# Key and value projections of a windowed attention moved into the steps of the compressed attention

## What is computed

```python
y_cmp = _mha(Q, blk, blk, ...[0])          # every query against 49 block means
y_sel = _mha(Q, K_sel, K_sel, ...[1])      # every query against the 4 best blocks
padded = jnp.pad(feat, ((0, 0), (pad, pad), (pad, pad), (0, 0)), mode='edge')
q = _lin(Q, wq_w[2], wq_b[2])              # query projection
k = _lin(patches, wk_w[2], wk_b[2])        # key projection, of padded positions
v = _lin(patches, wv_w[2], wv_b[2])        # value projection, of padded positions
attn = jax.nn.softmax(jnp.einsum('bnhd,bnwhd->bnhw', q, k) * scale, axis=-1)
y_win = _lin(jnp.einsum('bnhw,bnwhd->bnhd', attn, v).reshape(Bx, Nq, C), pj_w[2], pj_b[2])
g = jax.nn.softmax(_lin(_ln(Q, n1_w, n1_b), g_w, g_b), axis=-1)     # three gates per query
y = g[..., 0:1] * y_cmp + g[..., 1:2] * y_sel + g[..., 2:3] * y_win + Q
```

## Time and profile before

| | us |
|---|---|
| median of 3 runs (lowest, highest) | 842.41 (840.88, 844.82) |
| the profiled execution | 849.34 |
| its span | 847.5 |
| projection loop, first product to last | 92.12 to 224.4 |
| end of the gates | 234.5 |
| compressed attention, first maximum to last addition | 236.92 to 387.1 |
| windowed attention, then MLP | to 847.5 |

### The profile page before, as it was taken

How to read it: one execution, slowest core, us unless ns; L and a number is a source line. 1 busy time by engine, 2 the same in 40 slices (tenths; PEclk the granted TensorE clock), 3 DMA queues, 4 the chain that set the end, 5 groups by cost and what they waited for, 6 DMA issues and landing times.

```text
span 847.5 us, 14128 instructions
## 1 busy us (share of the span) xinstructions
PE 718.2 (85%) x5053; PEld 374.7 (44%) x5053; DVE 623.4 (74%) x1260; ACT 354.4 (42%) x609; POOL 201.4 (24%) x323
## 2 busy tenths in 40 slices
PE   4937966877489999997899899999988999999993
PEld 2525532333134444444455555555534545455551
DVE  6976445555677999996767767777729889999960
ACT  2160224434423344341445454454561351546566
POOL 1010122323324444440610010010056046600000
PEclk9966798999867999997799999999999999999998
DMA  5000055555588000001455665665100000000000
GB/s 223 0 1 0 19 141 126 143 145 135 139 201 220 1 0 1 2 0 56 124 147 142 164 172 135 173 165 150 37 4 1 0 0 1 1 19 20 38 39 38
DMA packets 52519, 66.22 MB, mean 78 GB/s; under 512 B 10590, under 2 KB 48226, under 8 KB 50594
## 3 DMA queue, kind: packets, MB, share of 16 engines
q1 hardware_dynamic: 49282, 43.08, 19.0%
q10 hardware_dynamic: 3168, 22.24, 9.5%
HBM read 43.03 MB, written 21.57 MB: 76 GB/s over the span
## 4 chain that ended last, share of the span: by engine, by line
PE 40%; DVE 20%; issue 5%; DMA 5%; ACT 4%; SPq 0%; POOL 0%; ACTq 0%; DVEq 0%
PE banks L870 12%; PE banks L810 5%; PE banks L794 5%; PE banks L772 4%; DVE mx L1241 4%; DVE sm L1254 3%; DMA Q<-nT 3%; PE banks L825 3%; DVE AC L1073 2%; DVE wn L1298 2%; DVE sm L1256 2%; DVE X L1326 2%; DMA FP<-nT 1%; PE banks L711 1%; PE banks L756 1%
## 5 line engine op out<-in xcount | busy, mean ns | idle before, releaser
L972 ACT ACTIVATE P<-banks 126x480 f32<-126x480 f32 (+2 forms) x196 | 100.2, 521 | 126.4 <-PE banks L794 102.3
L1298 DVE TENSOR_REDUCE wn<-banks 128x4 f32<-128x728 f32 x112 | 102.0, 914 | 40.6 <-PE banks L772 39.5
L870 PE MATMUL banks<-FP,PTB 128*128 128x392 f32 x384 | 129.5, 493 | 2.1 <-DVE c L1329 1.2
L1073 DVE SCALAR_TENSOR_TENSOR AC<-XT,vec,AC 128x1540 f32<-128x1540 f32 (+5 forms) x48 | 117.9, 2461 | 1.1
L870 PEld LDWEIGHTS banks<-FP,PTB 128*128 128x128 f32 x384 | 72.7, 190 | 56.8 <-DVE FP L1367 2.1
L501 POOL TENSOR_TENSOR SEB<-SEB,rg 112x392 f32<-112x392 f32 x112 | 58.3, 541 | 90.2 <-DVE rg L1261 90.1
L485 POOL TENSOR_TENSOR pk<-pr,pk 128x434 bf16<-128x434 f32 (+1 forms) x42 | 42.7, 1018 | 136.7 <-DVE pk L1181 136.7
L810 PE MATMUL banks<-P,Vw 126*17 126x120 f32 (+2 forms) x1568 | 74.3, 263 | 0.0
L1170 DVE TENSOR_TENSOR pr<-pf,pk 128x434 f32<-128x434 f32 (+1 forms) x42 | 31.9, 760 | 57.1 <-ACT pk L927 56.6
L951 ACT ACTIVATE SEB<-SEB 112x424 f32<-112x424 f32 x56 | 31.2, 557 | 89.8 <-DVE SEB L1244 89.8
L731 PE MATMUL banks<-PTB,VP 106*128 106x448 f32 x112 | 54.2, 572 | 5.1 <-ACT PTB L960 5.1
(11 more groups left out here) (228 smaller groups left out, 1255.3 us busy)
## 6 DMA issues: line engine op xcount, KB each, us to landing
k_parts<-pk SPq DMA_DIRECT2D x84, 108.5 KB, 2.8
Vw<-v_rows SPq DMA_DIRECT2D x84, 66.9 KB
q_parts<-pk SPq DMA_DIRECT2D x42, 112.0 KB, 2.7
K<-k_parts ACTq DMA_DIRECT2D x7, 651.0 KB, 6.0
v_rows<-vst SPq DMA_DIRECT2D x14, 263.5 KB
X<-in_x SPq DMA_DIRECT2D x2, 1568.0 KB, 8.1
out_y<-zs SPq DMA_DIRECT2D x8, 392.0 KB, 2.3
K<-k_parts ACTq DMA_DIRECT2D x7, 434.0 KB, 3.6
```

The costliest lines, as they stand in the source:

```text
L870: last = mm(bank(2 + place_in_unit, C, ZPIX), WT[:, dy, part, C * grp:C * (grp + 1)], D[:, part, QROWS * q + dy:QROWS * (q + 1) + dy, :].r ...
L972: a(P[q % 4][0:BKEYS[b], 0:4 * BQ[b]], PS[0:BKEYS[b], 4 + q % 2, 0:4 * BQ[b]], ACT.Exp).then_inc(sem("w_exp"), 1)
L1073: return ve.scalar_tensor_tensor(out=o, in0=src(ro + dy, rn, co + dx, cn), scalar=v(wcol + t), in1=o, op0=ALU.mult, op1=ALU.add)
L1298: ve.tensor_reduce(dst, src, AX.X, ALU.max, negate=True).then_inc(sem("w_slot_read"), 1)
```

## The change

The order of `pjobs` is turned round: 14 query jobs come first, then the 28 key jobs. Only the query jobs stay ahead of the compressed attention, one with each gate job. The loop there has 16 turns: in turn n, query job n and gate job n begin, gate job n-1 gets its two products, and gate job n-2 is transposed. The 28 key jobs are handed out over the first 40 of the 56 steps (`late_at[14 + n] = n * 40 // 28`, so in steps 0, 1, 2, 4, 5, 7, 8, 10, ...), always into bank 6. 16 of these steps also carry a value job (steps 0, 1, 4, 7, 10, 11, 14, 17, 20, 21, ...), in bank 7. For the job of step k, PE multiplies at the end of its step k, ACT reads at the end of its step k, DVE subtracts at the start of its step k+1 and rounds at its end (behind the value rows), and POOL makes the third part in its step k+2. SP stores these 28 jobs after it has spread the gate rows, and loads the first three bands after that. POOL clears borders only after its last step.

```diff
-        pjobs = [(m, "k", h * KBAND // 2, KBAND // 2) for m in range(IMAGES) for h in range(2 * BANDS)]
-        pjobs += [(m, "q", b * BAND, BAND) for m in range(IMAGES) for b in range(BANDS)]
+        pjobs = [(m, "q", b * BAND, BAND) for m in range(IMAGES) for b in range(BANDS)]
+        pjobs += [(m, "k", h * KBAND // 2, KBAND // 2) for m in range(IMAGES) for h in range(2 * BANDS)]
...
-        VPLACES = sorted([3 * k + 1 for k in range(NGJ)] + [2, 5])
+        NLATE = NPJ - NGJ
+        LATE_STEPS = 40
+        late_at = {NGJ + n: n * LATE_STEPS // NLATE for n in range(NLATE)}
+        vlate_at = {late_at[NGJ + j * 7 // 4]: j for j in range(NVJ)}
+        VPLACES = [NGJ + j * 7 // 4 for j in range(NVJ)]
...
-        PBANKS = (5, 6, 3)
+        PBANKS = (5, 7, 3)
+        LATE_BANK = 6
...
+                    for n in late_jobs(CB * i + k - 2):
+                        third_part(n)
...
-            c_body(0, False)
+            for i in range(BANDS):
+                c_body(i, False)
+            c_body(BANDS, True)
             pool.wait_ge(sem("proj"), NPJ)
...
-            for i in range(1, BANDS):
-                c_body(i, False)
-            c_body(BANDS, True)
...
+                    step = CB * i + k
+                    for n in late_jobs(step):
+                        pe.wait_ge(sem("proj_read"), n)
+                        if n == NGJ:
+                            pe.wait_ge(sem("g_rows"), 1)
+                        project(n, LATE_BANK)
+                    if step in vlate_at:
+                        values(vlate_at[step])
...
+                    for n in late_jobs(CB * i + k):
+                        first_parts(n, LATE_BANK)
...
+                    for n in late_jobs(CB * i + k - 1):
+                        residual(n)
...
+                    if CB * i + k - 1 in vlate_at:
+                        value_rows(vlate_at[CB * i + k - 1])
+                    for n in late_jobs(CB * i + k - 1):
+                        second_part(n)
```

More of the change, by code:

```diff
@@ L277, in build, with late_jobs @@
         NGJ = len(gjobs)
-        assert NPJ == 3 * NGJ
-        VPLACES = sorted([3 * k + 1 for k in range(NGJ)] + [2, 5])
-        assert len(VPLACES) == NVJ
+        NLATE = NPJ - NGJ
[3 more added lines that the diff above has]
+        VPLACES = [NGJ + j * 7 // 4 for j in range(NVJ)]
+        assert len(vlate_at) == NVJ and len(set(VPLACES)) == NVJ
+        def late_jobs(step):
+            return [n for n, at0 in late_at.items() if at0 == step]
         PEB = 5
-        PBANKS = (5, 6, 3)
+        PBANKS = (5, 7, 3)
+        LATE_BANK = 6
         CT = IMAGES * BANDS * TILES
@@ L381, in _, with store_parts @@
             sp.dma_start(pjrow[:], pjb).then_inc(sem("loaded"), 16)
-            for n, (m, which, at0, cols) in enumerate(pjobs):
+            def store_parts(n):
+                m, which, at0, cols = pjobs[n]
                 if n in VPLACES:
@@ L395, in _ @@
                     sp.dma_start(dst, pk[n % RING][:, part, 0:cols]).then_inc(sem(f"parts_stored{n % RING}"), 16)
+            for n in range(NGJ):
+                store_parts(n)
             sp.wait_ge(sem("g_rows"), 1)
@@ L401, in _ @@
                 sp.dma_start(SRG[SUBS * h:SUBS * (h + 1), :, :, :].rearrange("s i t n -> s (i t) n"), g_dram.rearrange("g s n -> s g n")).then_inc(sem("g_spread"), 16)
+            for n in range(NGJ, NPJ):
+                store_parts(n)
             for n in range(RING):
@@ L658, in by_query, with project @@
                 last.then_inc(sem("g_byquery"), 1)
-            for n, (m, which, at0, cols) in enumerate(pjobs):
-                if n >= 3:
-                    pe.wait_ge(sem("proj_read"), n - 2)
+            def project(n, b0):
+                m, which, at0, cols = pjobs[n]
                 if which == "k":
@@ L913, in _, with first_parts @@
             act.wait_ge(sem("c1"), 3)
-            for n, (m, which, at0, cols) in enumerate(pjobs):
+            def first_parts(n, b0):
+                m, which, at0, cols = pjobs[n]
                 act.wait_ge(sem("proj"), n + 1)
@@ new lines, in value_rows @@
+            def value_rows(j):
+                vm, g, k = vjobs[j]
+                dve.wait_ge(sem("vals"), j + 1)
+                if j >= 2:
+                    dve.wait_ge(sem(f"v_stored{j % 2}"), 16 * (j // 2))
+                o = vst[j % 2][:, 0:k, :].rearrange("p t (j d) -> p (t j) d", d=VH)[:, :, 0:DH]
+                i0 = PS[0:124, 7, 0:C * k].rearrange("p (t d) -> p t d", d=DH)
+                for t in range(k):
+                    last = ve.tensor_tensor(o[:, HEADS * t:HEADS * (t + 1), :], i0[:, HEADS * t:HEADS * (t + 1), :],
+                                            BV2[:].rearrange("p (j d) -> p j d", j=HEADS), ALU.add)
+                last.then_inc(sem("v_ready"), 1)
```

125 lines of the change are left out of this document (60 added, 65 removed).

## The result

| | before | after | ratio, 95% interval |
|---|---|---|---|
| median of 4 runs each | 843.62 us | 822.69 us | 0.9745 (0.9709 to 0.9781) |
| lowest and highest | 840.88, 847.2 | 819.6, 826.58 | |
| profiled execution (span) | 849.34 (847.5) | 820.55 (818.8) | |

What follows compares the result with a forecast made beforehand. The projection loop was taken as latency-bound, the compressed attention as full on DVE and PE. -80.0 + 66.2 = -13.8 us from the profiled 849.34 gave 835.5, less 6.9 for the median: 828.5, own range 818 to 839, overall 804 to 855.

Steps and rivals of the forecast that it cites:

- the port: First 40 steps: DVE's subtraction may lose 1.01 us to POOL's third part in 16 of 28 jobs; 8 us, ends 0 and 16.
- the clock's 8 us: First 40 steps: PE at half clock for 2.7 key steps, 3.0 us more each; 8 us, ends 0 and 16.
- turn of the projection loop: Projection loop: PE paces each of 14 turns at 3.65 us, 51.1 us in all.
- part 1: The shorter projection loop: gates ready 80.0 us earlier, ends 84 and 65.
- key step: Compressed attention: DVE waits for ACT's exponential, copy and two reads; 4.02 us for a step of 2.35, 28 times, 112.6.
- step without a key job: First 40 steps: 12 steps at 2.35 plus 0.33 us for the rounding of the job before, 2.68 each, 32.2.
- `XT`, exposed: First 40 steps: eight additions to `XT` of 0.54 us each, five taken as not hidden, 2.7 us.
- pairs and clock: First 40 steps: four pairs of value steps where PE waits for bank 7, 1.4 us each, 5.6; half clock, 8.
- 40 steps together: First 40 steps of the compressed attention: 169.1 us where they took 102.9, a cost of 66.2 us.
- Part 3: The rest: POOL's border clearing and the band loads stay hidden, loads needing at most 41 of 43.6 us.
- Half clock in the usual key steps: Rival, slower: PE at half clock in more than 7 of 28 key steps cancels the gain; 14 give 863; chance 0.18.
- DVE's own pace: Rival: ACT runs ahead, so a key job costs only DVE's work, 45 us with the clock; 807 us, chance 0.17.

Runs made afterwards that it cites:

- e8: The changed kernel with ACT's two reads of a key job put ahead of the exponential of the step: 810.12 us, ratio 0.9581.
- e10: e1 with ACT's two reads of a key job put ahead of the exponential of the step: 798.77 us, ratio 0.9442.
- e1: The changed kernel with the 16 value jobs given to key steps that are never neighbours: 818.02 us, ratio 0.9709.
- the second execution: The changed kernel, unaltered, run again in another session: 820.33 us, ratio 0.9712.
- e4: The kernel before, with only POOL's clearing of borders moved behind its last step: 843.67 us, ratio 1.0011.
- e3: e1 with DVE's subtraction of a key job also moved behind its gating of the step: 805.39 us, ratio 0.9558.
- e11: e10 with POOL's third part of a key job moved behind its normalization of the same step: 803.88 us, ratio 0.9509.
- e6: e1 with POOL's third part of a key job moved behind its normalization of the same step: 817.61 us, ratio 0.9683.

## Why the prediction was right

The direction, both large terms and the mechanism of each hold; the gain was 7 us larger than forecast. The small terms were less good: the port was put at 8 us and cost about nothing, and the clock's 8 us came in other steps than meant.

| term | forecast | measured |
|---|---|---|
| turn of the projection loop | 3.65 | 3.61 |
| part 1, first maximum earlier by | 80.0 | 84.1 |
| key step | 4.02 | 3.96 and 4.06 |
| step without a key job | 2.68 | 2.62 |
| `XT`, exposed | 2.7 | 3 x 0.88 + 2 x 0.41 = 3.5 outside the pairs and step 27 |
| pairs and clock | 5.6 + 8 | 13.4 in four pairs |
| port | 8 | about 0 |
| 40 steps together | 169.1 | 162.5 |

- **Part 1.** PE sets the pace of the loop, as the sum said. The 4.1 us more came from its ends: I gave start and filling 4.5 us and the way to the gates 6.7, together 11.2; of the 58.2 us to the gates 14 x 3.6 = 50.4 are turns, 7.8 are left. The measured 84.1 lies at the upper end, 84.
- **The key step.** Its path over exponential, copy and two reads was right to 0.06 us, and value rows and rounding hide in the wait (4.06 with them, 3.96 without). e8 and e10 show it from the other side: with the reads moved, the step is DVE's own work, 2.87, or 4.07 with value rows.
- **The pairs.** The place and the cause were right (e1), and so was the price of the wait: 1.4 us each were forecast, and the one pair that ran at full clock, step 1 of the second execution, took 1.4 over its neighbours. In the profile of after each of the four cost 3.3 to 3.5, since PE ran its products behind the wait at half clock, which the sum of a pair had left out. The 8 us for the clock were meant for usual key steps, and 13.4 - 5.6 = 7.8 us of half clock fell in these four. Two more steps had some: step 0 (4.75 here, 3.89 in the second execution) and step 27 (5.00, where e1 has 3.97), in which PE waited 2.13 us for ACT. That the two terms together, 13.6, met the 13.4 is luck in part: the 8 us were a middle between 0 and 16, and the working did not tie them to these waits.
- **The port.** This term of 8 us was mis-sized, at about 0 for DVE: its subtractions took 0.60 to 0.65. POOL was stretched instead, L502 from 1.01 to between 1.30 and 1.36 us in 16 of the 28 jobs, and nobody waits for it. The order in which the two meet was missing in my working: where the step before had a key job too, value rows or rounding keep DVE busy, and the subtraction starts ahead of the third part. e1 made the subtraction meet POOL at work, and it took 1.0 to 1.4 us more in each of four steps, where the earlier trace rows and the third part's length gave 1.01 as the price. The Trainium skill's rule ("SBUF — State Buffer", Who interferes with whom), that issue order decides, gave the right sum. e1's step 2 does not follow it as I read it, since the subtraction that started at 164.94 let a POOL instruction of 165.51 go ahead. Nor does e10's by its recorded starts, where POOL's instruction of 166.30 let the subtraction of 166.43 go ahead. Here the measurement decides.
- **The baseline.** The sum stood against the 849.34 of the profile, with 4.6 us of half clock in it that most likely belong to that execution (e4). Against the 98.04 of e4's 40 steps the change costs 64.4 there, and -84.1 + 64.4 = -19.7 is near the -20.9 of the medians. This is worked out, not shown.
- **Part 3.** The clearing is hidden, and so are the band loads: SP issues the first at 319.95, and the DMA engines fall silent near 356, more than 7 us ahead of the first product of the windowed attention. Busy time at the loads' end:

```profile
354.00:356.00 2.00, 1.01 (x5) 0.29 (x5) 1.86 (x8) 0.97 (x3) 1.04 (x2) 1.00 0.50 103
356.00:358.00 2.00, 1.77 (x11) 1.03 (x10) 0.17 (x1) 0.57 (x2) 1.75 (x9) 1.00 0.03 7
```

PE's row of that first product, which waits for DVE alone:

```profile
363.75 0.82 PE L805 MATMUL banks<-FP 126*64 126x182 bf16 x16 [1.91 <-DVE banks L1324]
```

- **The rivals.** Half clock in the usual key steps did not come: 0.91 over the 40 steps, by way of the pairs and steps 0 and 27. The Trainium skill's rule on loops that fall back to half clock at each wait ("TensorE: Matmul & The Clock Gate", HAM oscillation) fits the four waits for bank 7 in the profile of after, but not the second execution, where the clock stayed at 1.00 behind one of them, nor most of the shorter waits, as the rows in the last section tell. DVE's own pace (807) was held off by the reason given, the reads behind an exponential that waits for DVE; e8 takes the reason away and comes to 810, still with its pairs.

## What to carry to other kernels

When work is moved from a stage that waits into one that is full, sum one step of the full stage along the queue with the longest chain (here ACT: exponential, copy, two reads), not along the busiest engine. That queue's order is then what is left to gain: two instructions put ahead of one that waits for the other engine gave 12 us (e8), and 24 us with the value jobs spread (e10). Of two moved kinds of work, let no two instances of the one that shares a single bank stand in neighbouring steps, and put the exposed one into steps that have a wait to hide it.

## What the runs showed of the hardware

- A subtraction on DVE with both inputs in SBUF that started during a POOL instruction, with a second POOL instruction right behind, waited for both: 2.04 and 1.6 us in place of 0.61 (e1). Started ahead of POOL's third part it took 0.60 to 0.65, and that part 1.30 to 1.36 in place of 1.01 (after). Started 0.13 us behind POOL's normalization, with DVE's rounding just before it, it took 0.60 as well, and the normalization's first instruction 1.44 (e10) in place of 0.84. So DVE and POOL hold each other up where no semaphore stands between them, and the opening section's "only at semaphores" is too narrow.
- DVE's rounding from float32 to bfloat16 in SBUF meets POOL too: 0.91 to 1.09 in place of 0.38 (e3, e11), which the earlier trace rows had shown only for the subtraction.
- A gap of PE did not decide its clock by its length alone. In after it was at 0.50 with the products behind the waits of 2.38 to 3.30 us for bank 7 or fell during them; in the second execution the same wait of 2.38 us stood ahead of products at full clock (1.14 for the values), and behind the one of 3.30 the clock fell only after the values. A wait of 2.13 us in step 27 stood ahead of a fall in both. One of 2.17 us in step 6 did not in after, but did in e6, where step 7 took 6.60; one of 1.83 in step 4 did not in after, but did in the second execution (1.82, and 1.81 for a projection that takes 1.00). PE's gap of 0.60 us stood ahead of a fall in one execution of the kernel before and ahead of none in e4, whose steps differ from it only in POOL's clearing. PE's rows of after, in order of time; the first two ran at full clock (1.02 for two products of `VP`), the last at half (1.86):

```profile
174.95 1.00 PE L690 MATMUL banks<-FP,W 128*128 128x434 f32 x2 [1.83 <-ACT pk L962]
...
181.94 1.02 PE L756 MATMUL banks<-PTB,VP 106*128 106x448 f32 x2 [2.17 <-ACT PTB L996]
...
262.73 1.86 PE L756 MATMUL banks<-PTB,VP 106*128 106x448 f32 x2 [2.13 <-ACT PTB L996]
```
